# TensorE's order in every half: logits matmuls ahead of probability transposes and value product

## The reference

```
lat  = layer_norm(layernorm(x));  kv = concat(layer_norm(ctx), lat)      # 64 + 64 rows
q, k, v = lat @ Wq, kv @ Wk, kv @ Wv             # 16 heads of 64
alphas  = softmax(q @ k.T / 8, masked)           # 64 x 128 per head
x1  = x + concat_heads(alphas @ v) @ Wo
x2  = layernorm(x1)
dense = top-2 of sigmoid(x2 @ gate_w), normalised        # 8 experts
out = x1 + silu(x2 @ ws1) * (x2 @ ws3) @ ws2 + sum_e dense_e * expert_e(x2)
```

## Time and profile before

| | us |
|---|---|
| median of 3 runs | 1191.71 (1191.34 to 1192.8) |
| the profiled execution's own time | 1191.51 |
| its span | 1189.8 |
| TensorE busy | 1142.1 (96%) |
| VectorE, ScalarE, GpSimd busy | 905.7, 900.2, 670.1 |

### The profile page before, as it was taken

The page is one execution under the profiler, slowest core; times in us unless marked ns, Lnnn a source line. Parts: engine busy times, 40 slices in busy tenths (PEclk is TensorE's granted clock), DMA queues, the critical chain, the costliest instruction groups (busy, mean ns, idle before and its releaser), DMA issues.

```text
span 1189.8 us, 29786 instructions
## 1 busy us (share of the span) xinstructions
PE 1142.1 (96%) x9000; PEld 1087.4 (91%) x9000; DVE 905.7 (76%) x4095; ACT 900.2 (76%) x3180; POOL 670.1 (56%) x781
## 2 busy tenths in 40 slices
PE   6899999999999999999999999999999999999986
PEld 5899999999999999999999999999999999999976
DVE  4777787777787777787778787778787778777776
ACT  4988777777777877777877778777778777777761
POOL 5565565665565665555665555665656565656431
PEclk9999999999999999999999999999999999999999
DMA  6001110111110111011111001111001111001101
GB/s 162 19 10 37 31 30 24 42 41 42 27 33 25 42 41 42 24 29 31 42 42 42 19 24 42 42 41 42 20 24 42 42 42 41 20 23 28 28 23 33
DMA packets 64399, 42.61 MB, mean 36 GB/s; under 512 B 8944, under 2 KB 63856, under 8 KB 64240
## 3 DMA queue, kind: packets, MB, share of 16 engines
q1 hardware_dynamic: 63056, 39.66, 12.7%
q10 hardware_dynamic: 1184, 1.05, 0.3%
HBM read 36.25 MB, written 4.45 MB: 34 GB/s over the span
## 4 chain that ended last, share of the span: by engine, by line
PE 76%; POOL 9%; DVE 7%; issue 4%; ACT 3%; DMA 1%; SPq 0%; DVEq 0%; ACTq 0%; POOLq 0%
PE bank L788 15%; PE bank L790 15%; PE bank L789 15%; PE bank L850 14%; PE bank L830 9%; PE bank L794 5%; POOL probs L419 3%; DVE pT_lo L679 2%; POOL x_r L441 2%; POOL x L448 2%; ACT pT_hi L496 2%; PE bank L859 2%; POOL x L444 2%; DVE x L699 1%; PE bank L907 1%
## 5 line engine op out<-in xcount | busy, mean ns | idle before, releaser
L419 POOL TENSOR_TENSOR probs<-probs,rdenom 128x512 f32<-128x512 f32 x256 | 266.9, 1043 | 340.8 <-DVE rdenom L654 340.8
L523 ACT ACTIVATE probs<-logits,neg_max 128x128 f32<-128x128 f32 x1024 | 402.2, 413 | 0.5 <-DVE neg_max L646 0.5
L850 PEld LDWEIGHTS bank<-kvT,tT 128*128 128x128 f32 x2048 | 267.3, 191 | 22.3
L850 PE MATMUL bank<-kvT,tT 128*128 128x128 f32 x2048 | 269.3, 274 | 0.0
L679 DVE TENSOR_TENSOR pT_lo<-bank,pT_hi 128x512 fp32r<-128x512 f32 x256 | 175.2, 685 | 90.6 <-ACT pT_hi L496 82.7
L646 DVE CUSTOM_DVE_ANT_0 logits<-bank,mask_add 128x128 f32<-128x128 f32 x1024 | 232.3, 282 | 5.1 <-PE bank L850 4.9
L496 ACT CAST pT_hi<-bank 128x512 fp32r<-128x512 f32 x256 | 152.9, 597 | 80.9 <-PE bank L830 80.4
L523 ACT ACTIVATION_READ_ACCUMULATOR probs<-logits,neg_max 128x1 f32 x1024 | 213.3, 208 | 0.0
L483 ACT ACTIVATE h_tanh<-bank 128x256 f32<-128x256 f32 x160 | 61.3, 383 | 170.3 <-PE bank L790 164.0
L689 DVE TENSOR_TENSOR cT_lo<-bank,cT_hi 128x512 fp32r<-128x512 f32 x256 | 174.7, 682 | 0.3
L830 PE MATMUL bank<-ident,probs 128*128 128x128 f32 x1024 | 155.7, 275 | 20.0 <-POOL probs L419 20.0
(11 more groups left out here) (111 smaller groups left out, 2610.2 us busy)
## 6 DMA issues: line engine op xcount, KB each, us to landing
gates<-gates_dram SPq DMA_DIRECT2D x62, 256.0 KB, 4.1
kv_raw<-in_ctx SPq DMA_DIRECT2D x32, 128.0 KB, 2.8
kv_raw<-in_x SPq DMA_DIRECT2D x32, 128.0 KB, 2.8
mask_raw<-in_mask_BxS_ik SPq DMA_DIRECT2D x32, 128.0 KB, 3.5
x_res<-in_x SPq DMA_DIRECT2D x32, 128.0 KB, 3.2
out<-out_sb SPq DMA_DIRECT2D x32, 128.0 KB, 1.8
gates_dram<-g_denseT SPq DMA_DIRECT2D x124, 2.0 KB
wq_raw<-in_L_xattn_Wq SPq DMA_DIRECT2D x1, 512.0 KB, 4.9
```

The source lines that it names most:

```text
L419: nc.gpsimd.tensor_tensor(probs[n][:, :, :], probs[n][:, :, :], rdenom[n][:, :].unsqueeze(2).broadcast_to([P, PAIRS, P]), ALU.mult).then_i ...
L523: nc.scalar.activation(probs[n % 4][:, r, :], logits[n % 2][:, r, :], ACT.Exp, bias=neg_max[n % 2][:, r:r + 1], scale=-1.0, accum_out=deno ...
L850: last = nc.tensor.matmul(S_ps[k % 2][:, P * r:P * (r + 1)], tT[:, k % 4, hd:hd + 2, :], kvT[p][:, k % 4, :], start=True, stop=True)
```

## The change

In TensorE's stream the block S is moved up, ahead of PT and C. Every half with logits then runs S, PT, C, (kvT,) T, W and the rest. Nothing else is touched: the waits, the banks, and the instructions of the other engines are those of before. Line numbers of TensorE's stream move: S is L834, PT L842, kvT L860, `attnT` L897, the gate L908, `x2` L936.

```
                     if k == 7 and has(j, p, 3, NG):
                         expert_outputs(p, 1).then_inc(y_in_psum, 1)
+                    if has_half(j, p, k, 0):          # S
+                        ...
+                        last.then_inc(S_in_psum, 1)
                     if has_half(j, p, k, 3):          # PT
                         ...
                     if has_half(j, p, k, 4):          # C
                         ...
-                    if has_half(j, p, k, 0):          # S
-                        ...
-                        last.then_inc(S_in_psum, 1)
                     if k == 2 and has(j, p, -1, NG - 2):
```

More of the change, by code:

```diff
@@ L824, in frame @@
                         expert_outputs(p, 1).then_inc(y_in_psum, 1)
+                    if has_half(j, p, k, 0):
+                        if k == 0:
+                            pe.wait_ge(kvT_ready, i + 1)
+                        if k in (0, 4):
+                            pe.wait_ge(t_ready, e + 4)
+                        after(pe, logits_ready, PAIRS * (e - 1))
+                        for r in range(PAIRS):
+                            hd = 8 * (k // 4) + 2 * r
+                            last = nc.tensor.matmul(S_ps[k % 2][:, P * r:P * (r + 1)], tT[:, k % 4, hd:hd + 2, :],
+                                                    kvT[p][:, k % 4, :], start=True, stop=True)
+                        last.then_inc(S_in_psum, 1)
                     if has_half(j, p, k, 3):
@@ L840, in frame @@
                                 pT_lo[kl % 2][:, :]).then_inc(C_in_psum, 1)
[L842 to L852, removed]
                     if k == 2 and has(j, p, -1, NG - 2):
```

## The result

The changed kernel takes 1253.29 us (median of 4 runs, 1252.86 to 1254.61) against 1192.26 us before (4 runs beside it): 61.0 us or 5.1% slower, ratio 1.0511, 95% interval 1.0493 to 1.0529. The forecast was 1232 us with a range up to 1248. The direction was right and the waits stand where they were expected, but a third of the loss was missed.

What follows compares the result with a forecast made beforehand. The prediction took TensorE's work plus its unavoidable waits as the bound. Place A 13.5, Place B 20.6, Place C -7.7, Place D 14.0 and 0.8 at the end made +41.2 us on 1191.5, so 1232 us, range 1210 to 1248.

Steps and rivals of the forecast that it cites:

- Place B: At k=2, kvT waits for `g_exp`, which ends later behind `cT_hi`: +0.71 us a frame, 20.6 us in 29 frames.
- Place D: At k=6, the `attnT` transposes wait for ScalarE's later copy: +0.45 us a frame, 14.0 us in 31 frames.
- Place A: From k=7 to the gate at k=1, the chain from PT to `x2` and `probs` runs 0.81 later: +0.45 us a frame.
- Place C: At k=3, 4, 5, no new wait; each half saves a 0.08 us type switch: -0.24 a frame, -7.7 us in all.
- The sum: Over the whole run, the four places and the last frame's end add +41.2 us to 1191.5, giving 1232 us.
- Rival 1: At PT, TensorE's wait for `probs` goes because PT asks 0.81 later: faster, 1150 us; chance 0.06, partial forms included.
- Rivals 2 and 3: 2: kvT and `attnT` transposes lose nothing, 1195 us, chance 0.04; 3: their waits half as long, 1215 to 1223, chance 0.10.
- Rival 4: ScalarE's delay reaches places called free (T, F, VectorE at k=3 and 4), 0.5 a frame, or clock falls: 1248 us; chance 0.10.

## Why the prediction was wrong, step by step

- **What bounds the kernel**: right. The time is TensorE's work plus its waits; with the waits moved away it is 2.1 to 2.4% faster in either order.
- **Place B**: right. It costs +0.77 a frame against +0.71; alone +23.3 us against 20.6. Its cause is shown: with `g_exp` ahead, kvT doesn't wait.
- **Place D**: the mechanism was right; that the size agrees (0.46 against 0.45; alone +14.9 us against 14.0) is partly luck. S was 0.08 longer than assumed, the transposes take 0.06 more after a wait, and against these the hand-off from ScalarE was 0.05 and not 0.15, and `attnT` ended 0.86 and not 0.90 behind the start of `cT_hi`.
- **Place A**: the mechanism was right, the size off. +0.74 a frame (0.17 in k=7 and 0, 0.57 in k=1) against +0.45. The chain moved by 0.89 or 0.90, not 0.81 (`x2` at 7.11 against 7.02), S of k=1 again took 0.89, and the transposes 0.27 instead of 0.2: so PT of k=1 came at 8.33, not 8.09, and the gate at 11.45, not 11.22. That is +0.68; the last 0.06 lie behind the gate's start, since after a wait its four matmuls take 0.44 us to the next start (615.10 to 615.54) and before took 0.36 (621.75 to 622.11).
- **Place C, the step that failed**: "Each half saves the switch", -0.24 in all, and with it the 0.81 us for S in every place. There is no switch to save. I had split T after S into a first step of 0.20 and steps of 0.12, and S into 0.81. But the record of the matmul behind S begins early: it starts at 612.92, while the load of its weights lasts until 613.08 (behind C in the changed kernel the load, 605.45 to 605.64, is over before the matmul starts at 605.68). Its step is long by what S seems short, and 0.81 + 0.20 is 0.89 + 0.12. S is 0.89: in front of PT (603.65 to 604.54), in front of nothing new (k=3 still takes 4.16 us), and when doubled. The expert outputs, plain fp32 too, show it: 20 in 2.23 us (639.25 to 641.48), 0.11 each, and S is eight of them. The weight load in question and, from the chain of waits of the kernel before, which I had read for its stations and not for its sizes, the right figure for S:

```profile
612.89 0.19 PEld L788 LDWEIGHTS bank<-latT_hi,MV_hi 128*128 128x128 f32 x1
...
618.25 0.66 PE bank L830 x4
...
619.60 0.89 PE bank L850 x8
```

- **The sum.** With what was measured: A 0.74 x 30 = 22.2, B 0.77 x 29 = 22.3, C nothing, D 0.46 x 31 = 14.3, the end 0.8: 59.6 of the 61.0 us. The false step is worth 7.7 us in C. The 0.81 for S that goes with it is worth more: with 0.89 the prediction's own steps give +0.61 in A, +0.79 in B and +0.53 in D, which is 4.8, 2.3 and 2.5 us. Together that is 17.3 us, and the forecast would have been about 1250, 3 below the measured time. (The sum as written, 1191.5 and 41.2, makes 1232.7, so the forecast was also rounded the wrong way by a little.) The formula of the Trainium skill that I weighed against the rows ("TensorE: Matmul & The Clock Gate", Back-to-back issue gap) has the number of columns in it and nothing else; by it there was no saving, and the run with S ahead at k=3, 4, 5 bears that out. The section gives the formula for the isolated gap, though, and T's steps took 0.12 us here where it has 0.109.
- **Rival 1** (faster, the wait for `probs` goes) holds for k=1 alone: -3.7 us. It fails for k=7, where `probs` moves with PT, as the prediction had it. **Rivals 2 and 3** fall: B and D were paid in full. **Rival 4** (worse, by ScalarE's delay at places called free) gave the right time nearly, but not by its mechanism: k=2 to 5 are longer by 0.79, of which B is 0.77. The granted clock did not fall in the frames; the frame as a stretch of the changed kernel (columns as in the earlier trace rows), and nearly the whole run:

```profile
603.65:641.48 37.83, 35.71 (x281) 33.45 (x279) 28.05 (x127) 28.88 (x99) 20.90 (x25) 1.00 0.12 33
50.00:1230.00 1180.00, 1110.40 (x8628) 1038.79 (x8628) 871.74 (x3940) 899.80 (x3088) 637.65 (x733) 1.00 0.12 31
```

It stayed at 1.00. It did fall after the last full frames of this execution, and that is a loss that no place accounts for. One group of expert outputs there, in the kernel before and in the changed one:

```profile
1176.23 2.50 PE L794 MATMUL bank<-w_sb,h 128*128 128x128 f32 x20 [1.24 <-POOL h L428]
1237.37 4.63 PE L794 MATMUL bank<-w_sb,h 128*128 128x128 f32 x20 [1.11 <-POOL h L428]
```

From 1237.40 to 1240.80 the granted clock was 0.50, the lower level (1.2 GHz), where the kernel before kept 1.00 to its end; the 20 matmuls took 4.28 us to the next start, not 2.25. That is about what the profiled execution's 63.1 us exceed the 61.0 of the medians by. The change is not seen to cause it: TensorE's waits ahead of the fall are alike in both kernels (1.16, 0.38 and 1.29 us against 1.17, 0.36 and 1.29), and among the other kernels' profiles the fall comes in some and not in others. What does cause it stays open.

## What to carry to other kernels

A block that nobody waits for is not free to move ahead of one that others wait for: price it by what stands *behind* the delayed results in the consumers' queues (here `g_exp`, `attnT`, `x1`), not by the engine that moves. Where a busy engine waits, look first whether the awaited instruction stands behind an unrelated one in its producer's queue; two such moves gave 25 us, and the best orders of TensorE's blocks that were run gave only 3 to 4. Size a block by two of its kind in a row, or with different followers, before a saving is read from one step.

## What the runs showed of the hardware

Plain fp32 matmuls of 128 columns take 0.11 us each from start to start at the full granted clock (20 in 2.23 us, 8 in 0.89). An fp32r matmul of 256 columns behind them has its start recorded some 0.08 us early (0.81 in place of 0.89), and its follower then seems late (0.20 in place of 0.12); over both, nothing is lost. A group of matmuls that TensorE had to wait for takes 0.06 to 0.08 us more to the next start (0.28 against 0.22 for the `attnT` transposes, 0.44 against 0.36 for the gate). TensorE waiting four times a frame, up to about 1 us, did not lower its granted clock, which was 1.00 from 50 to 1230 us. In the tail of the same execution, behind waits of 1.16, 0.38 and 1.29 us, it fell to 0.50 and 20 matmuls took 4.28 us instead of 2.25; the kernel before had the same waits there and kept 1.00. So these rows do not settle when the clock falls.
